# A graph layer's last step: node group 0 is taken ahead of the sums of the last six places, and the node tiles are dealt out anew

## The reference

```python
h = gelu(x @ Wi.T + bi)
for i in range(L):                                   # L = 4
    res = h
    q, k, v = (h@Wq.T+bq)[dst], (h@Wk.T+bk)[src], (h@Wv.T+bv)[src]    # 8 heads of 16
    alpha = sum(q * k, -1) / 4
    ex = exp(alpha - segment_max(alpha, dst)[dst])
    a = ex / (segment_sum(ex, dst)[dst] + 1e-16)
    out = segment_sum(a[:, :, None] * v, dst)
    x_r = h @ Ws.T + bs
    beta = sigmoid(concat([out, x_r, out - x_r]) @ Wbeta.T)
    h = layer_norm(beta * x_r + (1 - beta) * out + res) * ln_g + ln_b
    h = gelu(h @ W1.T + b1) @ W2.T + b2 + h
x = layernorm(x + h @ Wo.T + bo)
```

## Time and profile before

| | before |
|---|---|
| median of 3 runs | 5648.73 us |
| the profiled execution's own time | 5648.17 us |
| its span (first to last record) | 5646.4 us |
| PE busy | 4297.1 us, 76% |
| DVE busy | 4045.0 us, 72% |
| ACT busy | 2765.2 us, 49% |
| POOL busy | 3847.5 us, 68% |
| mean granted TensorE clock | 0.763 of full |

### The profile page before, as it was taken

One profiled execution on the slowest core, in us unless ns is written; L12 is line 12 of the kernel. 1 busy time (PEld: TensorE's weight loads), 2 busy tenths in 40 slices (PEclk: granted clock), 3 DMA queues, 4 the chain that ended last, 5 costly groups with the idle time before them and its releaser, 6 DMA issues.

```text
span 5646.4 us, 105857 instructions
## 1 busy us (share of the span) xinstructions
PE 4297.1 (76%) x22799; PEld 3510.1 (62%) x22800; DVE 4045.0 (72%) x11127; ACT 2765.2 (49%) x6393; POOL 3847.5 (68%) x4061
## 2 busy tenths in 40 slices
PE   6777777777777777777777777777777677777776
PEld 4666666556666665566666655666666566666665
DVE  6878877768777777687777777777777754444445
ACT  1555555435555554455555554555555444444442
POOL 5777777447777773477777735777777347777775
PEclk7777776787776776877777678777676788888888
DMA  6444444234444442344444423444444212222221
GB/s 173 109 110 110 109 110 109 67 98 110 109 110 109 110 109 68 96 110 110 109 109 110 109 65 99 109 109 109 110 109 109 53 52 60 60 61 61 60 60 38
DMA packets 267185, 536.12 MB, mean 95 GB/s; under 512 B 116251, under 2 KB 148687, under 8 KB 266507
## 3 DMA queue, kind: packets, MB, share of 16 engines
q0 software_dynamic: 180992, 490.24, 32.8%
q1 hardware_dynamic: 78899, 35.89, 2.6%
q10 hardware_dynamic: 6936, 6.69, 0.3%
HBM read 512.41 MB, written 18.03 MB: 94 GB/s over the span
## 4 chain that ended last, share of the span: by engine, by line
POOL 63%; issue 24%; DVE 4%; PE 4%; POOLq 2%; DMA 2%; ACT 1%; SPq 0%; DVEq 0%; ACTq 0%
POOL slots L509 62%; PE bank L951 1%; DMA resets<-flat_rst 1%; PE bank L910 1%; PE bank L942 1%; POOLq L506 1%; POOLq L507 0%; DVE acc L1196 0%; PE bank L789 0%; DVE slots L1432 0%; POOLq L495 0%; DVE slots L1378 0%; DMA kv_table<-slots 0%; DVE slots L1438 0%; POOLq L501 0%
## 5 line engine op out<-in xcount | busy, mean ns | idle before, releaser
L509 POOL DMA_INDIRECT slots<-kv_table,idx x3224 | 3062.8, 950 | 1349.4 <-issue 980.6
L789 PE MATMUL bank<-slots,oh 128*128 128x136 f32 (+1 forms) x8060 | 1514.1, 337 | 322.0 <-DVE acc L1196 317.4
L770 PE MATMUL bank<-qs,ohT 128*128 x8080 | 1629.8, 347 | 110.0 <-ACT ohT L545 36.6
L789 PEld LDWEIGHTS bank<-slots,oh 128*128 128x128 f32 x8060 | 1334.1, 239 | 441.9 <-DVE acc L1196 395.6
L770 PEld LDWEIGHTS bank<-qs,ohT 128*128 128x128 f32 x8080 | 1382.4, 249 | 308.8 <-issue 286.7
L1196 DVE TENSOR_TENSOR acc<-acc,bank 128x136 f32 (+1 forms) x4030 | 1176.4, 292 | 531.3 <-PE bank L789 190.4
L545 ACT ACTIVATE ohT<-bank,miss 128x512 f32<-128x512 f32 x1010 | 678.3, 682 | 1180.2 <-PE bank L761 1178.8
L509 POOL DMA_INDIRECT slots<-src_table,idx x806 | 762.0, 945 | 378.7 <-issue 245.3
L554 ACT ACTIVATE oh<-iota,rel_e 128x128 f32<-128x128 f32 x3168 | 963.0, 387 | 0.0
L1213 DVE TENSOR_TENSOR slots<-slots,bank 128x512 f32<-128x512 f32 x808 | 552.8, 684 | 77.7 <-DMA slots<-kv_table,idx 72.7
L1288 DVE TENSOR_TENSOR slots<-slots,bank 128x544 f32<-128x544 f32 x808 | 577.5, 715 | 12.8 <-PE bank L838 2.7
(11 more groups left out here) (255 smaller groups left out, 3883.3 us busy)
## 6 DMA issues: line engine op xcount, KB each, us to landing
slots<-kv_table,idx POOLq DMA_INDIRECT x3224
kv_table<-slots SPq DMA_DIRECT2D x20, 660.0 KB, 3.4
slots<-src_table,idx POOLq DMA_INDIRECT x806
resets<-flat_len ACTq DMA_DIRECT2D x51, 128.0 KB
idx<-src_e SPq DMA_DIRECT2D x255, 8.0 KB
terms<-flat_rel SPq DMA_DIRECT2D x255, 12.0 KB
resets<-flat_rst SPq DMA_DIRECT2D x2, 1551.0 KB
w<-in_w SPq DMA_DIRECT2D x8, 256.0 KB, 4.1
```

What stands on the lines that cost most here:

```text
L509: pool.indirect_dma_start(slots[:, k, t, 0:width], None, table, bass.IndirectOffsetOnAxis(ap=idx[:, k, t:t + 1], axis=0))\
L770: mm = pe.matmul(o, ohT[:, j % 2, t, :], qs[:, blocks[j * G + t], 0:HID], start=True, stop=basis is None)
L789: mm = pe.matmul(bank[6 + part % 2][:, o:o + width], oh[:, k % 2, t, :], slots[:, k, t, HID:HID + width], start=True, stop=True)
```

## The change

In the last chunk's step of each layer, DVE now runs `attended`, `differences` and `mixed` of group 0 between the scaling of the open block and `weigh(0)`, `normed` of group 0 between the two `weigh`, and `attended` and `differences` of group 1 behind `weigh(1)`, before the six sums (`add`). PE now turns and expands group 0 ahead of the matmuls of the six places. ACT's program is unchanged. `contract` of group 0 gets a wait for the sums before its second half, because that half writes bank 6, which holds sums. So that node tiles can be written while the last chunk is still in `slots` and `oh`, they are dealt out anew: `t1`, `t2`, `dx`, `zT` into the first ring slot, `g1` of group 0 into the fourth, `spare`, `o_c[0]` and `den` to the end; `o_c[1]` and the others stay in `oh` behind the last chunk's six matrices. `den` and `rden` become one tile. Setup tiles get other offsets. No instruction is added or removed on DVE, ACT, POOL or SP's queues, nor on PE, beside the one wait.

```diff
@@ build_program @@
-        tsrc = rows_of(BW)
+        tsrc, t1, t2, dx = [rows_of(BW) for _ in range(4)]
+        zT = [node_tile(GW) for _ in range(2)]
+        assert at[0] <= CH * KVW
         kvst = rows_of(NB, KVW)
-        t1, t2, dx = rows_of(BW), rows_of(BW), rows_of(BW)
-        g1 = [node_tile(4 * GW).rearrange("p (f k) -> p f k", f=4) for _ in range(2)]
-        zT = [node_tile(GW) for _ in range(2)]
+        assert at[0] >= (2 * CH + LAST_PLACES) * KVW
+        g1 = [node_tile(4 * GW).rearrange("p (f k) -> p f k", f=4) for _ in range(2)][::-1]
...
-        o_c = [oh_f[:, i * GW:(i + 1) * GW].rearrange("p (b k) -> p b k", b=BW) for i in range(NI)]
-        spare = oh_f[:, NI * GW:(NI + 1) * GW].rearrange("p (b k) -> p b k", b=BW)
+        spare = rows_of(BW)
+        o_c = [rows_of(BW), *[oh_f[:, CH // 2 * P + i * GW:CH // 2 * P + (i + 1) * GW].rearrange("p (b k) -> p b k", b=BW)
+                              for i in range(NI - 1)]]
...
@@ tensor: attend_step @@
-                add_up(g, k, 0, HEADS * VW, w_done, g, last)
+                if last:
+                    pe.wait_ge(ld_layer, 64 * (l + 1))
+                    turn_rows(l, 0, last_layer)
+                    expand(l, 0, last_layer)
+                    add_up(g, k, 0, HEADS * VW, w_done, g, last)
+                    add_up(g, k, 1, HEADS * VW, w_done, g, last)
+                    return
+                add_up(g, k, 0, HEADS * VW, w_done, g)
...
@@ tensor: contract @@
                     pe.wait_ge(h_new, START + 2 * r)
+                    if i == 0 and s == 1:
+                        pe.wait_ge(acc_done, START + CH * CHUNKS * (l + 1))
...
@@ tensor: layer @@
                 for k in range(REM):
-                    attend_step(l, FULL, k, k < REM - 1)
-                pe.wait_ge(ld_layer, 64 * (l + 1))
-                turn_rows(l, 0, last)
-                expand(l, 0, last)
+                    attend_step(l, FULL, k, k < REM - 1, last)
@@ vector: attend_step @@
                 dve.tensor_tensor(a_0, a_0, bcl(scale[:, :], VW), ALU.mult).then_inc(acc_scaled, 1)
                 if ahead:
                     multiply(n, l, i_n, kn, 0)
+                if last:
+                    attended(l, 0, step)
+                    differences(l, 0, step)
+                    mixed(l, 0, step)
...
                 weigh(0)
                 if ahead:
                     sum_heads(n, kn, 0, groups_n)
+                if last:
+                    normed(l, 0, step)
                 weigh(1)
                 if ahead:
                     multiply(n, l, i_n, kn, 1)
+                if last:
+                    attended(l, 1, step)
+                    differences(l, 1, step)
...
@@ vector: layer @@
                 dve.wait_ge(acc_done, START + CH * CHUNKS * (l + 1))
                 if last:
                     dve.tensor_scalar(xn[:, :, 64], acc[:, :, DH], 0.5, None, ALU.is_ge)
-                attended(l, 0, step)
-                differences(l, 0, step)
-                mixed(l, 0, step)
-                normed(l, 0, step)
-                attended(l, 1, step)
-                differences(l, 1, step)
                 mixed(l, 1, step)
```

More of the change, by code:

```diff
@@ L200, in build_program @@
         out_rows = [kvst[:, i * BW:(i + 1) * BW, 64:P] for i in range(NI)]
-        den, rden = [oh_f[:, (NI + 1) * GW + i * BW * HEADS:(NI + 1) * GW + (i + 1) * BW * HEADS].rearrange("p (b h) -> p b h", b=BW)
-                     for i in range(2)]
+        den = rows_of(BW, HEADS)
         w02, w12 = sb("w02", [P, P]), sb("w12", [P, P])
@@ L211, in build_program @@
         su_o = flat_slots[:, 2 * TILES:3 * TILES]
-        row = flat_slots[:, 9000:9000 + 12 * (NB + 1)].rearrange("p (a b) -> p a b", a=12)
-        rowi = flat_slots[:, 9400:9400 + 4 * (NB + 1)].bitcast(I32).rearrange("p (a b) -> p a b", a=4)
-        vt = flat_slots[:, 9600:9600 + 4 * VC].rearrange("p (a b) -> p a b", a=4)
+        row = flat_slots[:, 10500:10500 + 12 * (NB + 1)].rearrange("p (a b) -> p a b", a=12)
+        rowi = flat_slots[:, 10900:10900 + 4 * (NB + 1)].bitcast(I32).rearrange("p (a b) -> p a b", a=4)
+        vt = flat_slots[:, 11100:11100 + 4 * VC].rearrange("p (a b) -> p a b", a=4)
         vti = sb("vti", [P, VC], I32)
@@ L223, in build_program @@
         r_prev = oh_f[:, 2700:2700 + VC * P].rearrange("p (c e) -> p c e", c=VC)
-        all_ones = flat_slots[:, 10400:10400 + P]
-        w_i = flat_slots[0:64, 10200:10200 + HID]
+        all_ones = flat_slots[:, 11900:11900 + P]
+        w_i = flat_slots[0:64, 11700:11700 + HID]
         r_next = r_ok
@@ L228, in build_program @@
         r_bf = flat_slots[:, 13000:13000 + VC * RW].bitcast(BF16).rearrange("p (i c e) -> p i c e", i=2, c=VC)
[L229 to L235, removed]
+        below, chosen, diagonal = [flat_slots[:, 12030 + m * 30:12030 + m * 30 + NB + 1] for m in range(3)]
+        full_rows, tail_count, head_count, total = [flat_slots[0:NB + 1, 12120 + m:12121 + m] for m in range(4)]
+        limit_row, limit = flat_slots[:, 12130:12130 + NB + 1], flat_slots[:, 12160:12161]
+        first_dst = flat_slots[:, 12161:12162]
+        r_src = flat_slots[:, 15000:15000 + VC * P].rearrange("p (c e) -> p c e", c=VC)
+        spread_f = flat_slots[0:3 * NG, 14000:14000 + NG * P].rearrange("p (j e) -> p j e", j=NG)
+        r_terms = flat_slots[:, 11300:11300 + 3 * VC * P // 2].bitcast(BF16).rearrange("p (f c e) -> p f c e", f=3, c=VC)
         r_near = flat_qs[:, 4 * VC * P:5 * VC * P].rearrange("p (c e) -> p c e", c=VC)
         r_sq = flat_qs[:, 5 * VC * P:6 * VC * P].rearrange("p (c e) -> p c e", c=VC)
-        edge_word = flat_slots[0:1, 9700:9702]
+        edge_word = flat_slots[0:1, 11200:11202]
         ld_const, ld_count, ld_rows, ld_layer, ld_dst = sem("ld_const"), sem("ld_count"), sem("ld_rows"), sem("ld_layer"), sem("ld_dst")
@@ L811, in turn_ends, with attend_step @@
                 mm.then_inc(rows_turned, 1)
-            def attend_step(l, i, k, ahead):
+            def attend_step(l, i, k, ahead, last_layer=False):
                 c = RING * i + k
@@ L844, in attend_step @@
                     rows(n, kn, 2, blocks, groups=groups)
-                add_up(g, k, 1, HEADS * VW, w_done, g, last)
-                if last:
-                    return
+                add_up(g, k, 1, HEADS * VW, w_done, g)
                 if ahead and groups > 2:
@@ L1257, in carries, with attend_step @@
                     .then_inc(shift_done, 1)
-            def attend_step(l, i, k, ahead):
+            def attend_step(l, i, k, ahead, step=None):
                 c = RING * i + k
@@ L1411, in attended @@
                 step(dve.tensor_scalar(den[:, :, :], sums[:, :, :, DH], 1e-16, None, ALU.add))
-                step(dve.reciprocal(rden[:, :, :], den[:, :, :]))
+                step(dve.reciprocal(den[:, :, :], den[:, :, :]))
                 step(dve.tensor_tensor(o_c[i].rearrange("p b (h d) -> p b h d", h=HEADS), sums[:, :, :, 0:DH],
-                                       bcl(rden[:, :, :], DH), ALU.mult))
+                                       bcl(den[:, :, :], DH), ALU.mult))
                 for b in range(BW):
@@ L1498, in layer @@
                 for k in range(REM):
-                    attend_step(l, FULL, k, k < REM - 1)
+                    attend_step(l, FULL, k, k < REM - 1, step)
                 dve.wait_ge(acc_done, START + CH * CHUNKS * (l + 1))
```

## The result

The changed kernel takes 5666.95 us (median of 9 runs, 5663.24 to 5670.9), the kernel before 5647.91 us (median of 9, 5645.83 to 5653.33). The ratio is 1.0033 with a 95% interval of 1.0024 to 1.0041: the change makes the kernel slower by 19 us, between 13.6 and 23.2. Forecast were 5671 us, 5657 to 5680.

The account below looks back on a forecast made before the run. The prediction took POOL's chain of gathers as the bound, with four gaps, one per layer, where a DVE-PE relay counts in full. 5648.17 + 14.85 (Term 1) + 8 (Term 2) = 5671.0 us; range 5664 to 5679, with A and B's edge 5657 to 5680.

Parts of the forecast that it names:

- POOL's waits: Between layers: the three waits for `kv_table` would sum to about 360 us, the one for `src_table` be near 140.
- The reserve: DVE, block's scaling to `normed` of group 1: four waits, 2.70 us together in layer 0, that the new order could fill.
- Term 1: DVE waits for the first sum, whose matmuls stand behind `expand` of group 0 on PE; +14.85 us over four layers.
- 6 to 7 us: Sign: idle time of DVE ahead of the last step's first sum, released by PE.
- over 8: Sign: the same idle time of DVE ahead of the first sum, in layer 3, in us.
- Term 2: PE idles 8 us before the turn of group 1 and runs on at half clock; +2.0 us a layer, 8 in all.
- The further 0.5 a layer: Part of Term 2 beyond +1.5: `expand` of group 1 starts cold and delays DVE's keys; 0.1 to 1.5 us left.
- A: Rival: only Term 1, PE's clock still up at the turn of group 1; 5663 us, chance 0.13.
- B: Rival: full clock in `expand` of group 0, or delay partly made up later; 5656.5 us, chance 0.07.
- C: Rival: places' matmuls done before DVE wants the sums, all 2.70 us of waits go; 5636.5 us, chance 0.05.
- D: Rival: no change, the growth of POOL's gap is hidden; chance 0.05.
- The costs of nothing: Claimed free: new tile places and setup offsets, `contract`'s new wait (met at 1111.2), POOL's and SP's untouched queues.

Follow-up runs that it names:

- e1: Changed kernel with the six places' matmuls on PE between the turn and `expand` of group 0; 5645.34 us, 0.9987 of the kernel before.
- e7: The changed kernel measured once more, unaltered, in a second set of runs; 1.0030 of the kernel before.
- e4: Changed kernel with 14 unread matmuls on PE in its pause before the turn of group 1; 1.0026 of the kernel before.
- e8: Changed kernel with 14 unread matmuls on PE ahead of the turn of group 0; 1.0023 of the kernel before.
- e9: e8 with ACT giving the eight gelus of group 0 ahead of the gate of group 1; 1.0015 of the kernel before.
- e3: Kernel before with only the new places of node and setup tiles, every engine's order as before; 5652.48 us, 1.0001 of the kernel before.
- e6: e1 with 9 unread matmuls (7 in layer 3) on PE before the turn of group 1; 5635.08 us, 0.9979 of the kernel before.
- e5: Changed kernel with 10 unread matmuls on PE ahead of the turn of group 0; 1.0031 of the kernel before.

## Why the prediction was right

**The total.** The two terms were 22.85 us in the forecast and 19.0 in the profiles, which is also the difference of the medians. That the profiled execution's 5670.9 us meets the 5671.0 forecast is luck: the terms were 3.8 us too large, and 3.7 us from outside of them filled the place. The same holds, in part, for POOL's waits (359.8 and 139.5 us, forecast 360 and 140), which contain 2.4 of these 3.7.

**The reserve, 2.70 us of DVE's waits a layer: right.** All four are gone, and e1's core of 27.5 confirms the work of 27.62 that was reckoned behind them.

**Term 1, the wait for the sums: right in kind, 2.3 us too large in sum (14.85 forecast, 12.5 measured).** By layer it was +3.75, +3.7, +2.5 and +4.9; measured +2.32, +3.24, +2.50 and +4.45. What was mis-sized is mainly `expand` of group 0. I carried its duration over from the same layer of before, 7.56 in layer 0, but it depends on the moment at which the clock rises, which comes anew in each execution: the changed kernel's row has 6.34, and e7's 7.23. The 1.22 us of difference there make most of the 1.43 missing in that layer, and over the four layers `expand` makes 1.4 of the 2.3. The remaining 0.9 is 0.2 to 0.3 us in each layer; in layer 0 `tsrc` is written 0.2 us sooner than reckoned, and the first sum starts 0.90 us behind the end of `expand` and not 1.10, less 0.2 for slightly longer work behind it. The links themselves came out: turn 0.13 us behind `tsrc`, `expand` 2.68 behind the turn. The sign "6 to 7 us" for the wait held in layer 1 alone (5.16, 6.10 and 5.35 us in layers 0 to 2); "over 8" held in layer 3 (8.05).

**Term 2, the clock behind `normed` of group 1: right, 8 forecast and 6.5 measured.** The pause is 9.0 us and not 8, the wait 3.18 and not 1.57, as forecast (+1.5, measured +1.61 a layer), and e4 shows that the clock makes all of it. The further 0.5 a layer for keys that come late is the part that was mis-sized; it didn't fall due. `expand` of group 1 takes 4.77 to 5.24 us in layers 0 to 2 instead of 4.57, since the clock is back soon after its start, and DVE's first product of the keys (`projected_keys`) starts 6.99 us behind `add_feed_forward`, as in before (7.00).

**The rivals.** A (term 1 only) falls with the rows at half clock. B wanted full clock in `expand` of group 0, and the changed kernel's turn of group 0 takes 1.32 us, half clock, with 0.50 granted until 1107; B took the core at full clock for +1.75 a layer in layers 0 to 2, and e8, which built that case, measured +1.1. B's other half, that the delay is made up later, isn't seen: the rest of the gap did not shrink (+1.1). C (faster) said that the sums would have to come before DVE wants them, and that is what e1 does by another order; with the order as changed, neither the clock (e8, a wait of 3.98 us) nor ACT's order with it (e9, 2.8 to 3.2) gets there. D falls with POOL's waits. The costs of nothing were right: e3 for the tiles, and `contract`'s new wait is met at 1113.1, ten microseconds before the turn.

Open stays where the 2.4 us of front and rest and the 1.3 us outside of the gaps are from. Their size is that of the scatter between layers. A kernel with DVE's order of before and PE's order of the change wasn't tried: PE would wait for `tsrc`, which DVE writes only behind the sums that PE has not yet made.

## What to carry to other kernels

When work is pulled ahead on one engine to fill its waits, ask of every engine in the relay what now stands in front of what the first one wants next: here 2.7 us of waits were filled and a wait of 5 to 8 us was made, because the partner's long block was put ahead of six short matmuls. Put the short piece that the other engine waits for ahead of the long one that nobody needs yet (e1). And where a new order leaves TensorE a longer pause (here 4 to 9 us), reckon its next stretch at half clock; 7 to 14 unread matmuls in the pause bought back 1.6 us a layer in the profiles of e4 and e6.

## What the runs showed of the hardware that I had not expected

The length of a pause alone did not tell whether TensorE came back at half clock. Behind the pauses of 3.99 to 11.2 us before the turn of group 0 or 1 it always did (the turn took 1.3 us). Shorter ones went either way. A pause of 2.63 us in e5, layer 0, was followed by half clock, while 2.42 us in layer 2 of the kernel before left it at full. Even equal pauses differed: in layer 3 PE idles 2.37 us ahead of the turn of group 2, and the turn took 0.77 us in the kernel before and 1.13 in e3, where the granted clock fell to 0.50 during it. The rows of before (layers 2 and 3), and that of e3:

```profile
3369.81 0.76 PE L933 MATMUL bank<-ident,slots 128*128 128x128 f32 x5 [2.42 <-DVE slots L1447]
...
4510.05 0.77 PE L933 MATMUL bank<-ident,slots 128*128 128x128 f32 x5 [2.37 <-DVE slots L1447]
```

```profile
4508.83 1.13 PE L934 MATMUL bank<-ident,slots 128*128 128x128 f32 x5 [2.37 <-DVE slots L1448]
```

Nor is one pause the whole of it: in layer 1 of e5 the clock was still up at the turn, after 2.00 us idle, and fell in the 1.35 us behind it. In e6 the unread matmuls covered all but 0.6 to 1.2 us, and the clock stayed up at the turn of group 1 in all four layers.

Keeping PE busy is not enough if it must wait on a partner behind that: e8 came to `expand` in layer 3 at full clock, did two tiles in 1.34 us, waited 2.10 for a gelu (the clock fell in that wait), and did the other six in 6.22 us where e9, waiting 0.50, took 4.19. The rows of e8:

```profile
4494.15 1.34 PE L951 MATMUL bank<-slots,w 128*128 128x320 f32 x4 [1.28 <-ACT slots L666]
4497.59 6.22 PE L951 MATMUL bank<-slots,w 128*128 128x320 f32 x12 [2.10 <-ACT slots L673]
```
